# A decoder layer: the mLSTM head norm's small steps on GpSimd, its row scales made column by column

## The reference, cut to what matters

```python
x = _layernorm(x + attention(x, ...))
x = _layernorm(x + mlstm(x, ctx, ctx, ...))
x = _layernorm(x + ffn(x, ...))
# inside the mLSTM, for each head:
    normalizer = jnp.maximum(jnp.abs(jnp.sum(C, axis=-1, keepdims=True)), jnp.exp(-max_log_D))
    h = jnp.einsum('bhst,bhtd->bhsd', C / (normalizer + EPS), vh)        # EPS = 1e-6
    mean = jnp.mean(h, axis=-1, keepdims=True)
    var = jnp.mean((h - mean) ** 2, axis=-1, keepdims=True)
    h_norm = (h - mean) * jax.lax.rsqrt(var + 1e-05) * outnorm_scale
# inside the feed-forward, for each row:
    scale = 127.0 / jnp.clip(jnp.max(jnp.abs(x), axis=-1, keepdims=True), 1e-05)
    xq = jnp.clip(jnp.round(x * scale), -128.0, 127.0) / scale
```

## Time and profile before

| | us |
|---|---|
| median of 3 runs | 715.84 (715.34 to 716.31) |
| profiled execution, its own time | 711.05 |
| its span in the trace | 709.3 |
| DVE busy | 618.5 (87% of the span) |
| PE busy | 614.1 (87%) |
| ACT busy | 566.2 (80%) |
| POOL busy | 506.6 (71%) |

### The profile page before, as it was taken

The page is one execution under the profiler, slowest core; times in us unless marked ns, Lnnn a source line. Parts: engine busy times, 40 slices in busy tenths (PEclk is TensorE's granted clock), DMA queues, the critical chain, the costliest instruction groups (busy, mean ns, idle before and its releaser), DMA issues. The chain is left out here.

```text
span 709.3 us, 16642 instructions
## 1 busy us (share of the span) xinstructions
PE 614.1 (87%) x4892; PEld 451.7 (64%) x4892; DVE 618.5 (87%) x2387; ACT 566.2 (80%) x1189; POOL 506.6 (71%) x781
## 2 busy tenths in 40 slices
PE   5578999999999999999999998999999979784642
PEld 4365676777768686867677675868676757552311
DVE  4466788999999999999999999999999999885853
ACT  3157978999898989888889988998989878966431
POOL 4176696969877887878888888888778865744322
PEclk9989999999999999999999999999999999997865
DMA  6999873465646462736556663846353641221101
GB/s 200 155 227 180 110 135 61 82 113 121 106 88 107 102 118 59 134 55 110 85 93 73 143 98 65 145 76 111 75 120 56 117 79 41 51 61 46 44 16 44
DMA packets 106104, 69.20 MB, mean 98 GB/s; under 512 B 47200, under 2 KB 106016, under 8 KB 106016
## 3 DMA queue, kind: packets, MB, share of 16 engines
q1 hardware_dynamic: 106016, 68.14, 53.0%
HBM read 28.73 MB, written 4.26 MB: 47 GB/s over the span
## 5 line engine op out<-in xcount | busy, mean ns | idle before, releaser
L1854 DVE CUSTOM_DVE_ANT_0 sc<-pS,bias 128x256 f32<-128x256 f32 x512 | 194.7, 416 | 26.9 <-PE pS L291 22.3
L1040 POOL TENSOR_SCALAR sc<-sc,mx 128x256 f32<-128x256 f32 x336 | 167.6, 511 | 12.1 <-DVE mx L1854 11.6
L1317 ACT ACTIVATE pr<-pT 128x512 f32<-128x512 f32 x256 | 147.5, 602 | 11.9 <-PE pT L309 10.9
L309 PE MATMUL pT<-ident,sc 128*128 128x128 f32 x1024 | 148.6, 275 | 7.0 <-ACT pr L1317 3.7
L309 PEld LDWEIGHTS pT<-ident,sc 128*128 128x128 f32 x1024 | 119.1, 142 | 26.2 <-issue 10.4
L291 PE MATMUL pS<-ks,qs 96*128 96x256 bf16 x512 | 93.1, 278 | 22.5 <-DVE mx L1854 16.6
L1305 ACT ACTIVATE sc<-sc,mx 128x256 f32<-128x256 f32 x176 | 84.1, 514 | 6.9 <-DVE mx L1854 6.9
L291 PEld LDWEIGHTS pS<-ks,qs 96*128 96x128 bf16 x512 | 44.5, 99 | 53.6 <-DVE mx L1854 31.9
L326 PE MATMUL pO<-pr,va 128*32 128x256 f32 x1024 | 68.5, 385 | 0.5 <-ACT oT L1327 0.5
L1007 POOL TENSOR_TENSOR rs<-ve,minus_half 128x2 f32<-128x2 f32 x48 | 34.3, 715 | 44.0 <-DVE ve L1885 43.7
L1062 POOL TENSOR_SCALAR hq<-h 128x512 bf16<-128x512 f32 x64 | 38.6, 621 | 30.7 <-ACT h L1516 28.7
(11 more groups left out here) (291 smaller groups left out, 1680.8 us busy)
## 6 DMA issues: line engine op xcount, KB each, us to landing
qs<-parts SPq DMA_DIRECT2D x96, 128.0 KB, 4.6
ks<-parts SPq DMA_DIRECT2D x96, 128.0 KB, 5.2
mb<-mrows SPq DMA_DIRECT2D x16, 512.0 KB, 3.9
xin<-in_x SPq DMA_DIRECT2D x16, 256.0 KB, 4.6
xb<-in_x SPq DMA_DIRECT2D x16, 256.0 KB, 3.4
cx<-in_ctx SPq DMA_DIRECT2D x32, 128.0 KB, 2.1
out<-hq SPq DMA_DIRECT2D x16, 256.0 KB, 2.3
bias<-in_L_attn_pos_bias SPq DMA_DIRECT2D x4, 768.0 KB, 8.0
```

The source lines that it names most:

```text
L309: ins = pe.transpose(bank[:, kt * S + t * P:kt * S + t * P + P], sc[:, s % RING, t, kt * P:kt * P + P], ident[:])
L1040: ins = pool.tensor_scalar(sc[:, s % RING, t, :], sc[:, s % RING, t, :], -1.0, mx[:, s % RING, t:t + 1], ALU.mult, ALU.add)
L1317: act.activation(flat(pr[:, s % RING, :, :]), pT[s % 2][:, :], ACT.Exp, scale=-1.0)\
L1854: dve.tensor_tensor_reduce(out=sc[:, s % RING, t, :], in0=pS[s % 2][:, t * S:t * S + S], in1=bias[:, s, t * P:t * P + S][:, ::-1], scale=1 ...
```

## The change

The eight small steps of the head norm that made sums, differences, squares and scaled sums move from DVE to one GpSimd function, head_moments, of nine instructions, which is written right in front of head_rstd in every batch; on DVE only the absolute value and the maximum stay (both now in head_bound). The mean's scaling moves: the sum under the root is four times as large as before, and head_norm multiplies by 2 to make up for it. head_centred now waits for the third of GpSimd's instructions, head_rstd for the ninth. The row clamp, the row scale and the two factors are made for one column (one tile t) at a time by tensor_scalar, with scalars in the place of the second tensor. Apart from the steps that vanish or are added, the orders on the engines stay as they were. The diff, cut to its core (the bodies of the removed DVE functions stand above; the order lists are shown for two batches):

```diff
-        gn_v, gn_g, ln2, x2_a = sig("gn_v", 16), sig("gn_g", 3), sig("ln2", 4), sig("x2_a", TT)
-        nm_v, yc_v = sig("nm_v", 3), sig("yc_v")
-        fq_v, xr_a, xq_g = sig("fq_v", 6), sig("xr_a", TT), sig("xq_g")
+        gn_v, hm_g, hn_v, gn_g, ln2, x2_a = (sig("gn_v", 8), sig("hm_g", 9), sig("hn_v"), sig("gn_g", 3), sig("ln2", 4),
+                                             sig("x2_a", TT))
+        nm_v, yc_v = sig("nm_v", 2), sig("yc_v")
+        fq_v, xr_a, xq_g = sig("fq_v", 10), sig("xr_a", TT), sig("xq_g")
...
+            def head_moments(f):
+
+                if not live(f):
+                    return
+                half = lambda k, part: hst[:, :, :, 3 * part + k]
+                pool.wait_ge(gn_v.sem, gn_v.at(f, 8))
+                pool.tensor_tensor(hmv[:, 1, :, :], half(1, 0), half(1, 1), ALU.subtract).then_inc(hm_g.sem, 1)
+                pool.tensor_tensor(hmv[:, 2, :, :], half(2, 0), half(2, 1), ALU.add).then_inc(hm_g.sem, 1)
+                wait(pool, yc_v, f - 1, 1)
+                pool.tensor_tensor(hmv[:, 0, :, :], half(1, 0), half(1, 1), ALU.add).then_inc(hm_g.sem, 1)
+                pool.wait_ge(nm_v.sem, nm_v.at(f, 2))
+                pool.tensor_scalar(nrm[:, 2, :, :], nrm[:, 1, :, :], 1e-6, 2.0 * 1e-5 ** 0.5, ALU.add, ALU.mult)\
+                    .then_inc(hm_g.sem, 1)
+                pool.wait_ge(hm_g.sem, hm_g.at(f, 1))
+                pool.tensor_tensor(hmv[:, 3, :, :], hmv[:, 1, :, :], hmv[:, 1, :, :], ALU.mult).then_inc(hm_g.sem, 1)
+                pool.wait_ge(hm_g.sem, hm_g.at(f, 2))
+                pool.tensor_scalar(hmv[:, 5, :, :], hmv[:, 2, :, :], 4.0 / XD, None, ALU.mult).then_inc(hm_g.sem, 1)
+                pool.wait_ge(hm_g.sem, hm_g.at(f, 4))
+                pool.tensor_tensor(nrm[:, 3, :, :], nrm[:, 2, :, :], nrm[:, 2, :, :], ALU.mult).then_inc(hm_g.sem, 1)
+                pool.wait_ge(hm_g.sem, hm_g.at(f, 6))
+                pool.tensor_tensor(hmv[:, 4, :, :], hmv[:, 3, :, :], hmv[:, 5, :, :], ALU.add).then_inc(hm_g.sem, 1)
+                pool.wait_ge(hm_g.sem, hm_g.at(f, 8))
+                pool.tensor_tensor(nrm[:, 5, :, :], hmv[:, 4, :, :], nrm[:, 3, :, :], ALU.add).then_inc(hm_g.sem, 1)
+
             def head_rstd(f):
 
                 if not live(f):
                     return
-                pool.wait_ge(gn_v.sem, gn_v.at(f, 15))
+                pool.wait_ge(hm_g.sem, hm_g.at(f, 9))
+                wait(pool, hn_v, f - 1, 1)
                 pool.tensor_tensor(nrm[:, 7, :, :], nrm[:, 5, :, :],
                                    minus_half[:, 0:TT * XH].rearrange("p (t h) -> p t h", t=TT), ALU.pow)\
                     .then_inc(gn_g.sem, 1)
...
-                pool.wait_ge(gn_v.sem, gn_v.at(f, 16))
+                pool.wait_ge(hn_v.sem, hn_v.at(f, 1))
                 pool.tensor_tensor(y2[:], y2[:], nw_bc[:, :].unsqueeze(1).to_broadcast([P, TT, D]), ALU.mult)\
                     .then_inc(gn_g.sem, 1)
...
                     wait(act, yc_v, c - 1, 1)
+                    wait(act, nm_v, c - 1, 2)
...
                 dve.wait_ge(cv_sb.sem, cv_sb.at(c, hh + 1))
+                wait(dve, hm_g, c - 1, 3)
                 for t in range(TT):
                     dve.bn_stats(hst[:, t, hh, :], cv[:, t, hh, 0:XD]).then_inc(gn_v.sem, 1)
 
-            def head_moments(f):
+            def head_bound(f, par):
 
                 if not live(f):
                     return
                 total = cv[:, :, :, XD]
...
                 dve.wait_ge(am_a.sem, am_a.at(f, 2))
-                dve.wait_ge(gn_v.sem, gn_v.at(f, 12))
+                dve.wait_ge(cv_sb.sem, cv_sb.at(f, XH))
+                wait(dve, hm_g, f - 1, 4)
+                dve.scalar_tensor_tensor(nrm[:, 0, :, :], total, -1.0, total, ALU.mult, ALU.max).then_inc(nm_v.sem, 1)
+                dve.wait_ge(nm_v.sem, nm_v.at(f, 1))
                 dve.tensor_tensor(nrm[:, 1, :, :], nrm[:, 0, :, :], emT[:, par, :, :], ALU.max).then_inc(nm_v.sem, 1)
-
...
-                dve.wait_ge(gn_v.sem, gn_v.at(f, 14))
+                dve.wait_ge(hm_g.sem, hm_g.at(f, 3))
...
-                dve.tensor_tensor(y, y, per_head(nrm[:, 7, :, :]), ALU.mult).then_inc(gn_v.sem, 1)
+                dve.scalar_tensor_tensor(y, y, 2.0, per_head(nrm[:, 7, :, :]), ALU.mult, ALU.mult).then_inc(hn_v.sem, 1)
...
                 dve.wait_ge(fq_v.sem, fq_v.at(f, 1))
-                dve.scalar_tensor_tensor(fs[:, 1, :], fs[:, 0, :], 1e-5, fs[:, 0, :], ALU.max, ALU.max).then_inc(fq_v.sem, 1)
+                for t in range(TT):
+                    dve.tensor_scalar(fs[:, 1, t:t + 1], fs[:, 0, t:t + 1], 1e-5, None, ALU.max).then_inc(fq_v.sem, 1)
 
             def row_inverse(f):
 
                 if not live(f):
                     return
-                dve.wait_ge(fq_v.sem, fq_v.at(f, 2))
+                dve.wait_ge(fq_v.sem, fq_v.at(f, 3))
                 dve.reciprocal(fs[:, 2, :], fs[:, 1, :]).then_inc(fq_v.sem, 1)
 
             def row_scale(f):
 
                 if not live(f):
                     return
+                dve.wait_ge(fq_v.sem, fq_v.at(f, 4))
+                for t in range(TT):
+                    dve.tensor_scalar(fs[:, 3, t:t + 1], fs[:, 2, t:t + 1], 127.0, None, ALU.mult).then_inc(fq_v.sem, 1)
+
+            def row_factors(f):
+
+                if not live(f):
+                    return
                 dve.wait_ge(fq_v.sem, fq_v.at(f, 3))
-                dve.scalar_tensor_tensor(fs[:, 3, :], fs[:, 2, :], -254.0, minus_half[:, 0:TT], ALU.mult, ALU.mult)\
-                    .then_inc(fq_v.sem, 1)
-
-            def row_factors(f):
-
-                if not live(f):
-                    return
-                dve.wait_ge(fq_v.sem, fq_v.at(f, 2))
                 wait(dve, th_a, f - 1, 4)
-                dve.scalar_tensor_tensor(fs[:, 5, :], fs[:, 1, :], w_gu[:, 3:4], minus_half[:, 0:TT], ALU.mult, ALU.mult)\
-                    .then_inc(fq_v.sem, 1)
-                dve.scalar_tensor_tensor(fs[:, 4, :], fs[:, 1, :], w_gu[:, 1:2], fs[:, 1, :], ALU.mult, ALU.mult)\
-                    .then_inc(fq_v.sem, 1)
+                for t in range(TT):
+                    dve.tensor_scalar(fs[:, 5, t:t + 1], fs[:, 1, t:t + 1], w_gu[:, 3:4], -0.5, ALU.mult, ALU.mult)\
+                        .then_inc(fq_v.sem, 1)
+                for t in range(TT):
+                    dve.tensor_scalar(fs[:, 4, t:t + 1], fs[:, 1, t:t + 1], w_gu[:, 1:2], fs[:, 1, t:t + 1], ALU.mult,
+                                      ALU.mult).then_inc(fq_v.sem, 1)
...
-                inner_quantised(3, 0); negated(6, 7); inner_quantised(3, 1); rstd(5, 0); head_rstd(4); negated(6, 8)
-                negated(6, 9); mem_scaled(4); mem_residual(4, 0); negated(6, 10); rstd(4, 1); negated(6, 11)
...
+                inner_quantised(3, 0); negated(6, 7); inner_quantised(3, 1); rstd(5, 0); head_moments(4)
+                head_rstd(4); negated(6, 8); negated(6, 9); mem_scaled(4); mem_residual(4, 0); negated(6, 10)
...
-                head_stats(6, 3); inner_factor(5, 1); biased(8, 8, 1); head_moments(6); attention_residual(7)
-                head_bound(6, 0); row_stats(7, 0); row_moments(7, 0); row_eps(7, 0); head_spread(6); head_floor(6)
-                head_variance(6); head_scale(6); biased(8, 9, 0); row_shift(7, 0); head_scaled(6); head_centred(6)
+                head_stats(6, 3); inner_factor(5, 1); biased(8, 8, 1); attention_residual(7); head_bound(6, 0)
+                row_stats(7, 0); row_moments(7, 0); row_eps(7, 0); biased(8, 9, 0); row_shift(7, 0); head_centred(6)
```

More of the change, by code:

```diff
@@ L1237, in from_batch_12 @@
                 negated(12, 6); inner_quantised(9, 0); negated(12, 7); inner_quantised(9, 1); rstd(11, 0)
-                head_rstd(10); negated(12, 8); negated(12, 9); mem_scaled(10); mem_residual(10, 0); negated(12, 10)
-                negated(12, 11); rstd(10, 1); input_rows(11); negated(12, 12); negated(12, 13); negated(12, 14)
-                negated(12, 15)
+                head_moments(10); head_rstd(10); negated(12, 8); negated(12, 9); mem_scaled(10); mem_residual(10, 0)
+                negated(12, 10); negated(12, 11); rstd(10, 1); input_rows(11); negated(12, 12); negated(12, 13)
+                negated(12, 14); negated(12, 15)
             def from_batch_13():
@@ L2442, in from_batch_15 @@
                 biased(15, 7, 0); head_stats(13, 1); biased(15, 7, 1); inner_bound(12, 1); biased(15, 8, 0)
-                head_stats(13, 2); head_stats(13, 3); inner_scale(12, 1); inner_factor(12, 1); head_moments(13)
-                attention_residual(14); head_spread(13); row_stats(14, 0); head_variance(13); row_moments(14, 0)
-                row_eps(14, 0); head_bound(13, 1); head_floor(13); head_scale(13); head_scaled(13); row_shift(14, 0)
-                head_centred(13); biased(15, 8, 1); biased(15, 9, 0); ffn_residual(12, 0); head_norm(13)
@@ L2452, in from_batch_15 @@
[L2452 to L2454 removed]
```

(16 more changed lines are left out.)

313 lines of the change are left out of this document (133 added, 180 removed).

## The result

| | before | after |
|---|---|---|
| median, us | 715.59 (714.76 to 716.31) | 740.49 (739.95 to 742.27) |
| profiled execution, its own time | 711.05 | 740.20 |
| DVE busy | 618.5 | 597.4 |
| POOL busy | 506.6 | 540.8 |

The ratio is 1.0352 (1.0324 to 1.038), 24.9 us on the medians; forecast were 10.0. The profiled executions differ by 29.1, since that of before was 4.5 us quicker than its median and that of after was not.

What follows compares the result with a forecast made beforehand. The prediction took DVE, busy 38.87 of 40 us, as the bound. Head_norm delays +16.8, vanished PE waits -2.6 and row steps -4.2 made +10.0 us on the median 715.84, so 725.8 us; range 710 to 743.

Steps and rivals of the forecast that it cites:

- what is put on it or taken off it ... is worth its full length: DVE in the 13 steady batches: about 1 us idle in 40, so added or removed work counts in full.
- earlier rstd: GpSimd's rstd behind row_eps: starts sooner because DVE has fewer steps, giving back 11.1 us over 13 batches.
- vanishing waits on PE: DVE right behind head_norm: small waits for PE vanish, -0.2 x 13 = -2.6 us.
- The price of the path: GpSimd from rstd to head_norm: nine steps and extras add 2.37 us a batch.
- The small step: One 128x8 GpSimd instruction ahead of the power: 0.19 us, nine cost 1.71 us.
- The two dependent pairs: GpSimd's last sum and power each wait for the instruction just before: 0.12 us each, 0.24 together.
- Meeting head_centred: A GpSimd instruction in the new chain is lengthened where it meets head_centred: 0.38 us once a batch.
- The emptying part: Batches f = 13 to 15: delays of 2.0, about 2.0 (some 0.8 reaching the end) and 1.7 us.
- Costed at nothing: GpSimd work behind the nine, some 1.3 us later, is covered by PE's and ACT's ring; without cover, +17 us.
- The row steps: DVE's clamp, scale and factors: 1404 ns a batch instead of 1668, -4.2 us in all, between nothing and -9.3.
- B: Rival at the DVE-GpSimd hand-over: cheap small GpSimd steps, DVE keeps its savings, faster; 703 to 714.4 us, chance 0.20.
- A: The forecast: DVE waits at head_norm for GpSimd's longer path, steps 0.13 to 0.30 us; 717.5 to 741 us, chance 0.62.

Runs made afterwards that it cites:

- nine_idle: Kernel before, all DVE steps kept, plus nine unused 128x8 GpSimd steps between rstd and the power: 749.49 us, ratio 1.0499.
- heads_only: The change without its row part (kernel after with before's four row functions): 743.0 us, ratio 1.0405.
- pe_less: Kernel before with 8 of 16 projection matmuls of each batch left out on PE: 716.32 us, ratio 1.0019.
- pe_less_steps_gone: Kernel before with half the projection matmuls and the eight small DVE head-norm steps left out: 710.3 us, ratio 0.9919.
- steps_gone: Kernel before without the eight small DVE head-norm steps and with none in their place on GpSimd: 711.92 us, ratio 0.9965.
- rows_only: Kernel before with only the row part of the change (clamp, scale, two factors by single columns): 710.52 us, ratio 0.9951.
- nine_behind: Kernel before with nine unused GpSimd steps put behind mem_residual instead of ahead of the power: 741.85 us, ratio 1.0383.
- four_idle: Kernel before with four unused small GpSimd steps between rstd and the power: 724.2 us, ratio 1.0132.

## Why the prediction was right in sign and wrong in size

The sum by stretches, in the time from one head_norm to the other, on the profiled executions:

| stretch | forecast | measured |
|---|---|---|
| up to head_norm(0) | 0.56 - 0.2 - 0.26 = +0.1 | 113.96 - 111.23 = +2.7 |
| head_norm(0) to head_norm(12) | 11.7 - 2.4 - 3.1 = +6.2 | 474.16 - 456.42 = +17.7 |
| head_norm(12) to the end | 4.5 - 0.8 = +3.7 | 150.28 - 141.65 = +8.6 |
| sum | +10.0 | +29.1 (24.9 on the medians) |

- **"what is put on it or taken off it ... is worth its full length" failed** for what is taken off, and with it two credits, 11.1 us for an earlier rstd and 2.6 for vanishing waits on PE. I read DVE's 38.87 of 40 as the bound. The Trainium skill (Perfetto Trace Analysis, section Identifying the Most-Contended Engine) reads a profile so too: the engine with the highest occupancy, for DVE also a fair measure of how near it is to its limit, is to be relieved first. Here the measurement differs, and it decides: 13.2 us less on DVE from 100 to 600 us gave 2.7. Together 13.7 were forecast; with the long path the eight steps are worth 35.7 - 29.2 = 6.5 (nine_idle against heads_only, so net of head_centred's new wait), and 2.7 without it. This is 7.2 of the 15 us by which the head part was off (29.2 against 16.8 - 2.6 = 14.2).
- **The earlier rstd** came in part only: GpSimd's idle time ahead of it (f = 0 to 12) fell from 12.8 to 9.6 us, where the forecast took 11.1 off. In f = 0 attention_residual, which stands ahead of row_eps, waits for PE's output projection and starts when it did before, and rstd starts at 108.37 where 106.61 was forecast (108.02 in before). First before, then after:

```profile
105.94 0.68 DVE L2160 TENSOR_TENSOR y<-pC,xb 128x512 f32<-128x512 f32 x1
```

```profile
105.97 0.69 DVE L2143 TENSOR_TENSOR y<-pC,xb 128x512 f32<-128x512 f32 x1 [0.72 <-PE pC L371]
```

It waits so 14 times in after, 5.9 us in all (once in before, 0.3). With half of the projection matmuls left out it waits in none, and then leaving out the eight steps takes 6.9 us off GpSimd's idle time ahead of rstd (12.7 in pe_less, 5.8 in pe_less_steps_gone) instead of 3.1 (12.8 in before, 9.7 in steps_gone): this wait held a good part of the credit. In f = 8 there is no such wait, yet GpSimd still stands 0.39 us ahead of rstd, 0.70 before; what held DVE there is not shown.
- **The waits on PE behind head_norm** did vanish, but their time did not come back. From the end of head_norm to row_stats DVE is idle 0.2 to 0.6 us a batch in before, in none of the batches f = 0 to 11 of after. But row_stats waits for mem_residual, which in most batches ends 2.7 us behind head_norm in both kernels, and DVE now stands there. In f = 8, first before, then after:

```profile
418.76 0.42 DVE L1854 CUSTOM_DVE_ANT_0 sc<-pS,bias 128x256 f32<-128x256 f32 x1 [0.17 <-PE pS L291]
...
419.46 0.75 DVE L1866 BATCH_NORM_STATS2 st<-y 128x6 f32<-128x256 f32 x2
```

```profile
433.42 0.75 DVE L1894 BATCH_NORM_STATS2 st<-y 128x6 f32<-128x256 f32 x2 [0.29 <-POOL y L1146]
```

From the end of head_norm to row_stats it took 38.4 us in these 13 batches and takes 39.9 now. So this stretch costs 1.5 us more where 2.6 less were forecast.
- **The price of the path was too low**: without the credits the forecast had 16.8 + 11.1 = 27.9, and nine_idle shows 35.7; these are the other 7.8. The small step was right, 0.16 to 0.17 us where 0.19 was forecast. The two dependent pairs were right too (0.28 and 0.27 where 0.31 was forecast). What I missed are the changes between TENSOR_TENSOR and TENSOR_SCALAR, some 0.11 us each, four in a batch, one of them behind the step that meets head_centred. The path is 2.60 us in nine_idle and 2.69 in after, in place of 2.33 (2.37 less 0.04); 0.27 us by 16 batches are 4.3 of the 7.8, and the rest no run prices by itself.
- **Meeting head_centred** cost 0.72 - 0.20 = 0.52 us in f = 8, where 0.38 was taken from the earlier trace rows. The step started at 426.77 and ended at 427.49, just behind head_centred's end at 427.38. This is what the Trainium skill (SBUF — State Buffer, section Who interferes with whom) says, that the second waits until the first is done; the trace agrees, and the term is then what is left of head_centred when they meet.
- **The emptying part** was off by 4.9. There the waits at head_norm grew from 0.00, 0.29 and 1.53 us (f = 13 to 15) to 2.07, 2.88 and 3.15, and the chain goes through all three powers; I had let 0.8 of f = 14 reach the end.
- **"Costed at nothing": mem_scaled 1.3 us later.** I named PE and ACT with their ring of heads as the cover and left out DVE's own row_stats behind mem_residual, whose wait grew by 6.9 us. Measured from head_norm, mem_scaled comes 0.4 to 0.8 us later in three of the 13 batches (f = 4, 9 and 10), where two or three negated steps stand between the power and it; in the others most of the grown wait is the one just told.
- **The row steps were right**: -3.3 (rows_only) for -4.2. (All four of the old steps read two tensors in SBUF, two of them by naming the same tile twice, and not three, as the description of the kernel says.) The steps save less than 0.26 us (0.15), because the factor with two scalars from SBUF takes 265 ns and not 206. And the stall went where it was said to go: the scan is 351 ns longer. In f = 4 of after the clamp takes 0.22 us, and the scan 1.74 beside GpSimd's addition (279.33 for 1.26 us), as the clamp and that addition did before.
- **The rivals**: B fell, since steps cost 0.16 and more and not 0.12; the figures of the Trainium skill (GPSIMD Engine Reference, section Elementwise — side-by-side cycle accounting), from which I had estimated 0.08 us a step, gave half of what the trace shows. A was the mechanism. Its upper end, 741, was reached not by steps of 0.30 us but about half by credits that did not come (7.2 us) and half by a path dearer for other reasons (7.8). That 740.5 still lies in the range 710 to 743 is therefore luck: its upper part was drawn for dearer steps.
- **What would show it**: DVE's idle time before head_norm was to be 1.5 to 2.5 us a batch and 20 to 30 in all: it is 1.5 to 3.2 and 32.4, with the power as releaser. The sign that was to tell that DVE is not the bound, a time that falls, did not come, and yet DVE was not the bound: only leaving its steps out showed that.

## What to carry to other kernels

A high busy share is no price list: where several engines with hand-written orders are level, work taken off one of them may return a fifth of its length, as here (2.7 of 13.2 us), while work put on it, and a longer hand-over, cost nearly their full length in every batch. So price what a moved step adds to the path between two semaphores in full, free length aside, and give no credit for what it takes off the busiest engine until leaving it out has been timed. Ask for each saving what its engine must wait for next, in order.

## What the runs showed of the hardware that I had not expected

- A 128x8 sum on GpSimd lasts 0.20 to 0.21 us and takes 0.16 from start to start. Two things add some 0.12: a wait for the step just before it, and a change between TENSOR_TENSOR and TENSOR_SCALAR. The second was not a wait: in nine_behind the TENSOR_SCALAR of L1088 waits for nothing and yet comes 0.28 us after L1087. A wait for a step two places back costs nothing: in four_idle L1088 waits for L1085 and comes 0.16 us after L1086.

```profile
438.41 0.20 POOL L1087 TENSOR_TENSOR dum<-minus_half 128x8 f32<-128x8 f32 x1
438.69 0.20 POOL L1088 TENSOR_SCALAR dum<-minus_half 128x8 f32<-128x8 f32 x1
```

```profile
419.74 0.20 POOL L1086 TENSOR_TENSOR dum<-minus_half 128x8 f32<-128x8 f32 x1
419.90 0.20 POOL L1088 TENSOR_TENSOR dum<-dum 128x8 f32<-128x8 f32 x1
```

- A DVE tensor_scalar on one column has three prices by its scalars: 145 ns with constants, 204 with one from SBUF, 265 with two.
- Half of PE's projection work less (37.6 us of 477 in the steady part) bought nothing, and the mean granted clock over the span was 0.929 to 0.947 in the ten executions of pe_less, 0.939 to 0.958 in the 25 of before beside them.
